# High parts of the self-attention's weights cast on ScalarE in place of GpSimd, with the block sums and the late rows' second round moved

## The reference

```python
x = _layernorm(x + _L0_attn_ref(...));  x = _layernorm(x + _L0_xattn_ref(...))
x = _layernorm(x + _L0_ffn_ref(...))
x = _layernorm(x + _L1_attn_ref(x, L1_attn_weight_qkv, L1_attn_weight_proj), axis=-1)   # here
x = _layernorm(x + _L1_xattn_ref(...)); x = _layernorm(x + _L1_ffn_ref(...))

def _L1_attn_ref(tokens, weight_qkv, weight_proj):
    SEQ, BATCH, HIDDEN = (512, 1, 1024)
    NUM_HEADS, NUM_KV_HEADS, HEAD_DIM = (32, 8, 128)
    Q_PER_GROUP = NUM_HEADS // NUM_KV_HEADS
    ...
    S, B, H = tokens.shape
    qkv = jnp.einsum('sbh,ph->sbp', tokens, weight_qkv)
    qkv = qkv.reshape(S, B, NUM_KV_HEADS, Q_PER_GROUP + 2, HEAD_DIM)
    ...
    scores = jnp.einsum('bhsd,bhtd->bhst', q, k) * scale
    scores = jnp.where(causal, scores, jnp.finfo(scores.dtype).min)
    attn = jax.nn.softmax(scores, axis=-1)
    out = jnp.einsum('bhst,bhtd->bhsd', attn, v)
    out = out.transpose(2, 0, 1, 3).reshape(S, B, NUM_HEADS * HEAD_DIM)
    return jnp.einsum('sbe,he->sbh', out, weight_proj)
```

## Time and profile before

| | |
|---|---|
| median of 3 runs | 3434.92 us (3430.94 to 3437.0) |
| the profiled execution's own time | 3445.45 us |
| its span, first to last instruction | 3443.7 us |
| self-attention, about | 790 to 2745 us of the span |
| TensorE matmuls busy, whole span | 3101.1 us (90%) |
| VectorE, ScalarE, GpSimd busy | 2116.8, 1378.1, 1436.0 us (61%, 40%, 42%) |
| TensorE's mean granted clock | 0.944 of full |

### The profile page before, as it was taken

How to read it: one execution, slowest core, us unless ns; L and a number is a source line. 1 busy time by engine, 2 the same in 40 slices (tenths; PEclk the granted TensorE clock), 3 DMA queues, 4 the chain that set the end, 5 groups by cost and what they waited for, 6 DMA issues and landing times. The chain is left out here.

```text
span 3443.7 us, 70284 instructions
## 1 busy us (share of the span) xinstructions
PE 3101.1 (90%) x26232; PEld 2571.2 (75%) x26232; DVE 2116.8 (61%) x4937; ACT 1378.1 (40%) x3762; POOL 1436.0 (42%) x1423
## 2 busy tenths in 40 slices
PE   5999999984789889988989899999999789999997
PEld 4888888772677778777867787878777568888886
DVE  6788888865454555555554354434444568888886
ACT  3778887763211111111111011101111177787774
POOL 3222222212664656466556766676676300111010
PEclk9999999985899999999989999999999989999999
DMA  9777777622121221122144212121121476656551
GB/s 284 191 189 189 190 190 188 177 74 74 56 71 44 77 71 62 59 89 77 44 162 181 80 56 68 50 68 65 63 77 37 186 180 158 159 148 156 149 139 44
DMA packets 233107, 397.97 MB, mean 116 GB/s; under 512 B 31185, under 2 KB 160817, under 8 KB 232258
## 3 DMA queue, kind: packets, MB, share of 16 engines
q1 hardware_dynamic: 229312, 391.27, 40.3%
q10 hardware_dynamic: 3458, 2.20, 0.2%
HBM read 296.97 MB, written 96.42 MB: 114 GB/s over the span
## 5 line engine op out<-in xcount | busy, mean ns | idle before, releaser
L879 DVE CUSTOM_DVE_ANT_0 L_masked<-L_scores,L_nmask 112x375 f32<-112x375 f32 x1024 | 552.6, 544 | 176.0 <-PE L_scores L483 138.1
L750 ACT ACTIVATE L_probs<-L_masked,L_least 112x375 f32<-112x375 f32 x1024 | 627.9, 615 | 81.1 <-DVE L_least L879 77.2
L1577 PE MATMUL sa_banks<-both_hi,sa_r_hi 128*128 128x420 f32 (+1 forms) x1344 | 500.2, 372 | 47.1 <-POOL sa_r_lo L1430 34.4
L488 PEld LDWEIGHTS L_turned<-ident_sb,L_probs 112*125 112x125 f32 x3072 | 458.2, 190 | 107.6 <-issue 48.0
L488 PE MATMUL L_turned<-ident_sb,L_probs 112*125 112x112 f32 x3072 | 527.3, 281 | 7.4 <-ACT L_probsT L745 3.3
L1910 DVE TENSOR_TENSOR sa_acc<-sa_acc,sa_banks 128x512 f32<-128x512 f32 x448 | 306.9, 687 | 337.8 <-PE sa_banks L1631 336.6
L1577 PE MATMUL sa_banks<-both_lo,sa_r_hi 128*128 128x420 f32 (+1 forms) x1344 | 490.2, 365 | 0.0
L1577 PE MATMUL sa_banks<-both_hi,sa_r_lo 128*128 128x420 f32 (+1 forms) x1344 | 489.5, 364 | 0.0
L1430 POOL TENSOR_TENSOR sa_r_lo<-sa_raw,sa_r_hi 128x512 fp32r<-128x512 f32 (+1 forms) x304 | 466.8, 1536 | 45.2 <-issue 2.3
L483 PE MATMUL L_scores<-L_krep,L_qrep 128*112 128x376 f32 x1024 | 418.6, 410 | 8.4 <-DMA L_qrep<-query_parts 6.6
L745 ACT COPY L_probsT<-L_turned 125x336 f32<-125x336 f32 x768 | 337.3, 439 | 177.4 <-PE L_turned L488 169.2
(11 more groups left out here) (317 smaller groups left out, 5532.5 us busy)
## 6 DMA issues: line engine op xcount, KB each, us to landing
L_qrep<-query_parts SPq DMA_DIRECT2D x256, 224.0 KB, 6.1
sa_raw<-in_wqkvU_dram SPq DMA_DIRECT2D x192, 256.0 KB, 3.2
L_krep<-ctx_parts SPq DMA_DIRECT2D x256, 188.0 KB, 4.2
sa_raw<-in_wprojU_dram SPq DMA_DIRECT2D x128, 256.0 KB, 3.0
query_parts<-L_qT_hi SPq DMA_DIRECT2D x64, 224.0 KB, 6.4
query_parts<-L_qT_lo SPq DMA_DIRECT2D x64, 224.0 KB, 6.8
L_xcur<-x SPq DMA_DIRECT2D x32, 448.0 KB, 5.0
L_val<-in_ctx_dram SPq DMA_DIRECT2D x64, 187.5 KB
```

The source lines that it names most:

```text
L488: mm = pe.transpose(turned[0:TC, m % 2, S * j:S * j + S], probs[0:S, m % 4, TC * j:TC * j + TC], ident[0:S, 0:S])
L750: nc.scalar.activation(probs[0:S, e % 4, :], masked[0:S, e % 4, :], ACT.Exp, bias=least[0:S, e:e + 1], scale=-1.0, accum_out=rsum[0:S, e:e ...
L879: v.tensor_tensor_reduce(out=masked[0:S, n % 4, :], in0=scores[0:S, (NH * t + n) % 3, 0:T], in1=nmask[0:S, :], scale=1.0, scalar=HUGE, op0 ...
L1577: mm = pe.matmul(out_of[o][:, 0:width], a[:, n % RING, k, :], right, start=(o in opens and i == 0), stop=(i == 3 * HALF_KT - 1), skip_grou ...
```

## The change

Four things change, all within `self_attention`; the arithmetic stays the same.

1. The casts of all weights' high parts (pairs and heads) go from GpSimd to ScalarE: `cast_weight(n)` and `cast_head(G, hp, j)`. GpSimd keeps the subtraction (`low`) and waits for the cast with a new semaphore, `cast_ok`; `cast_at` numbers the casts in ScalarE's order. The casts stand in ScalarE's order by `follow(G, pr, o)`: behind the `keep` of product o comes the cast for product o + 4; where heads follow the pair, the casts of the two heads take the places at `B21` and `T3`, and the first four weights of the *next* pair are cast at `T4` (one) and `B22` (three), ahead of `weighted`.
2. GpSimd's block sums stand earlier: a21 + a22 ahead of the first weight of a pair, and the other three each behind the subtraction that they follow. ScalarE waits for them with `mix_ok`.
3. The late rows' second round goes from the pair Q01 to behind the heads: on ScalarE and VectorE it stands within `project(G, 0)`, at chunks 0 to 3.
4. SyncE stores the second round's parts one group later, just ahead of the raw loads of the next group's Q01, and loads the next late row behind them.

```diff
--- before.py
+++ after.py
...
+        def weight_source(G, pr):
+            first = place[G, units(pr)[0], None, 0]
+            a11, a21, a22, a12 = (raw[:, (first + i) % 6, :] for i in range(4))
+            return [x.rearrange("p (k n) -> p k n", k=HALF_KT) for x in (a11, mid[:], mid[:], a12, a11, a22, a12)]
...
                 if u == Q_UNIT + 2 and r is not None:
-                    for n in range(2):
-                        store_parts(r, n)
-                if (u, j) == (None, 0) and r is not None and r + 1 < NC:
-                    load_late(r + 1)
+                    store_parts(r, 0)
+                if u == (K_UNIT if G == NKV else Q_UNIT) and G and late_row(G - 1) is not None:
+                    store_parts(late_row(G - 1), 1)
+                    if r is not None:
+                        load_late(r)
...
-            def split(hi, lo, src, done):
-                p.tensor_copy(hi, src)
-                pool.drain()
+            def low(hi, lo, src, key, done):
+                pool.wait_ge(cast_ok, cast_at[key])
                 p.tensor_tensor(lo, src, hi.bitcast(F32), ALU.subtract).then_inc(done, 1)
 
             def weights(G, pr, start=0, stop=OPS):
                 hi, lo = ring_of(G)
-                ua, ub = units(pr)
-                first = place[G, ua, None, 0]
+                first = place[G, units(pr)[0], None, 0]
                 a11, a21, a22, a12 = (raw[:, (first + i) % 6, :] for i in range(4))
-                source = (a11, mid[:], mid[:], a12, a11, a22, a12)
+                source = weight_source(G, pr)
                 for o in range(start, stop):
                     n = OPS * (3 * G + pr) + o
-                    if n >= RING:
-                        pool.wait_ge(prod_ok, n - RING + 1)
                     if o == B11:
                         loaded(first)
+                        loaded(first + 2)
+                        p.tensor_tensor(mid[:], a21, a22, ALU.add).then_inc(mix_ok, 1)
+                    low(hi[:, n % RING, :, :], lo[:, n % RING, :, :], source[o], ("w", n), w_ok)
                     if o == T1:
-                        loaded(first + 2)
-                        p.tensor_tensor(mid[:], a21, a22, ALU.add)
-                    if o == T2:
                         pool.drain()
-                        p.tensor_tensor(mid[:], mid[:], a11, ALU.subtract)
-                    if o == T3:
+                        p.tensor_tensor(mid[:], mid[:], a11, ALU.subtract).then_inc(mix_ok, 1)
                         pool.drain()
-                        p.tensor_tensor(a11, a11, a21, ALU.subtract)
-                        p.tensor_tensor(a12, a12, mid[:], ALU.subtract)
-                    pool.drain()
-                    split(hi[:, n % RING, :, :], lo[:, n % RING, :, :],
-                          source[o].rearrange("p (k n) -> p k n", k=HALF_KT), w_ok)
+                        p.tensor_tensor(a11, a11, a21, ALU.subtract).then_inc(mix_ok, 1)
+                    if o == B21:
+                        pool.drain()
+                        p.tensor_tensor(a12, a12, mid[:], ALU.subtract).then_inc(mix_ok, 1)
                     if o in (T3, T4, B22):
                         pool.drain().then_inc(raw_free, 2 if o == T3 else 1)
...
             def heads(G, hp):
...
                 hi, lo = heads_of(G, hp)
                 for j in range(2):
-                    split(hi[:, j, :], lo[:, j, :], raw_of(G, None, 2 * hp + j), p_ok)
+                    low(hi[:, j, :], lo[:, j, :], raw_of(G, None, 2 * hp + j), ("p", G, 2 * hp + j), p_ok)
                     pool.drain().then_inc(raw_free, 2)
...
+            def cast_weight(n):
+                m, o = n // OPS, n % OPS
+                G, pr = m // 3, m % 3
+                first = place[G, units(pr)[0], None, 0]
+                if o == B11:
+                    loaded(first)
+                if o == B21 or o == T1:
+                    loaded(first + 2)
+                if o in (T1, T2):
+                    act.wait_ge(mix_ok, 4 * m + o)
+                if o in (T3, B22):
+                    act.wait_ge(mix_ok, 4 * m + 4)
+                if n >= RING:
+                    act.wait_ge(prod_ok, n - RING + 1)
+                if G == NKV and pr == KV and o < RING:
+                    act.wait_ge(proj_ok, heads_done(G - 1, 0))
+                nc.scalar.copy(ring_of(G)[0][:, n % RING, :, :], weight_source(G, pr)[o]).then_inc(cast_ok, 1)
+
+            def cast_head(G, hp, j):
+                if j == 0 and ends_half(G) and hp:
+                    act.wait_ge(prod_ok, OPS * 3 * (G + 1))
+                elif j == 0 and nth[G, hp]:
+                    G0, hp0 = projects[nth[G, hp] - 1]
+                    act.wait_ge(proj_ok, heads_done(G0, hp0))
+                i = place[G, None, 2 * hp + j, 0]
+                loaded(i)
+                nc.scalar.copy(heads_of(G, hp)[0][:, j, :],
+                               raw[:, i % 6:i % 6 + 2, :].rearrange("p x n -> p (x n)")).then_inc(cast_ok, 1)
+
+            def follow(G, pr, o):
+                n = OPS * (3 * G + pr) + o
+                last = pr == Q23 and ends_half(G)
+                owner = (G - 1, 1) if pr == Q01 and late_project(G) else (G, 0) if pr == Q23 else None
+                if o % 2 == 0 and o < B22:
+                    keep(G, pr, o // 2)
+                if owner is None or o < B21:
+                    cast_weight(n + RING)
+                elif o in (B21, T3):
+                    cast_head(*owner, o - B21)
+                elif not last:
+                    cast_weight(n + 2)
+                if owner and o == B22 and not last:
+                    cast_weight(n + 3)
+                    cast_weight(n + 4)
+
...
+                    if hp == 0 and c == 2 and late_row(G) is not None:
+                        high_parts(1, late_row(G), 1)
+                    if ends_half(G) and hp == 0 and c in (3, 4):
+                        cast_head(G, 1, c - 3)
+                    if last and c == 1 and G + 1 < GROUPS:
+                        for first in range(RING):
+                            cast_weight(OPS * 3 * (G + 1) + first)
...
-                keep(G, KV, 0)
-                if late_project(G):
-                    take_exp(G - 1, 1)
-                keep(G, KV, 1)
-                keep(G, KV, 2)
-                if r is not None:
-                    norm(EARLY1 + r, late[:], norm_ok)
-                keep(G, Q01, 0)
-                if r is not None:
-                    copy_turned(1, r)
-                    high_parts(1, r, 0)
-                keep(G, Q01, 1)
-                keep(G, Q01, 2)
-                if r is not None:
-                    high_parts(1, r, 1)
+                for o in range(OPS):
+                    follow(G, KV, o)
+                    if o == T1 and late_project(G):
+                        take_exp(G - 1, 1)
+                    if o == T4 and r is not None:
+                        norm(EARLY1 + r, late[:], norm_ok)
+                for o in range(OPS):
+                    follow(G, Q01, o)
+                    if o == B11 and r is not None:
+                        copy_turned(1, r)
+                        high_parts(1, r, 0)
                 if late_project(G):
                     weighted(G - 1, 1)
-                keep(G, Q23, 0)
-                values(G)
-                take_exp(G, 0)
-                keep(G, Q23, 1)
-                keep(G, Q23, 2)
+                for o in range(OPS):
+                    follow(G, Q23, o)
+                    if o == B11:
+                        values(G)
+                    if o == T1:
+                        take_exp(G, 0)
                 weighted(G, 0)
...
+                    if hp == 0 and c == 0 and late_row(G) is not None:
+                        differences(1, late_row(G), 1)
+                    if hp == 0 and c == 3 and late_row(G) is not None:
+                        low_parts(1, late_row(G), 1)
...
-                combine(G, Q01, 0)
-                if r is not None:
-                    differences(1, r, 1)
-                combine(G, Q01, 1)
-                if r is not None:
-                    low_parts(1, r, 1)
-                combine(G, Q01, 2)
-                combine(G, Q01, 3)
+                for n in range(4):
+                    combine(G, Q01, n)
```

21 lines of the change are left out of this document (13 added, 8 removed).

## The result

The changed kernel takes 3570.6 us (median of 4 runs, 3566.0 to 3574.3) against 3436.0 (4 runs, 3430.9 to 3437.6): 3.9% slower, ratio 1.039 (95% interval 1.038 to 1.041).

A forecast was written before the change was run, and what follows sets the result against it. TensorE was taken as the bound, so only its waits count. Terms 31 + 55 + 7 + 9 - 3 + 1 + 1.5 + 26 = 128 us gave 3573 on the profiled 3445.5, or 3563 on the median 3434.9; range 3510 to 3625.

The forecast's parts named there:

- What goes: Ahead of products at T3: TensorE's 34.4 us of waits for GpSimd's low parts should be gone without GpSimd's casts.
- The new wait: Projections after Q23: `weigh` held by ScalarE's queued casts, +5.2 us each in groups 1 to 6, +9.1 in 9 to 14.
- K + 11.7: Start of the second `weigh` after the change, 11.7 us behind K, the start of ScalarE's third `kept` copy.
- Late row: Projection after Q01, groups 1 to 7: `weigh` +1.3 us later each (-0.8 to +2.6), 9 us in all.
- The second round in `project(G, 0)`: ... 0: Late row's three casts and three subtractions moved into that projection: no cost, at most 1 us for seven groups uncovered.
- +1, with ScalarE held once in `project(7, 1)`: Group 8: the expert block's delay less three T3 waits, +1 us in all, ScalarE held once in that projection.
- Clock: The 12 projections after Q23: mostly at full clock before, not after the longer waits, 2.2 us each, 26 us.
- The start: Start of the stage: GpSimd's first block waits for ScalarE, which delays the first roots, +1.5 us.
- ScalarE is not held, faster: Rival: casts ahead of the projection find `mid` ready, so existing waits and low clock shrink, 3296 us; 5%.
- The second rival: Raw loads in late groups and expert blocks hide: late groups take 15 us less, second half 35 less, 3513 us; 12%.
- the third: Rival: low clock lasts longer, or ScalarE is late for `kept` in late groups, 3616 us; 23%.
- The fourth: Rival: gains at T3 and in the late groups equal the added wait, so time stays at 3435 us; 3%.

The follow-up runs named there:

- e1: The changed kernel with the casts of T2 and B21 moved behind the casts into `o_hi` of chunk 3: 3437.2 us, 0.999 of the kernel before.
- e2: The changed kernel with T1's cast behind `o_hi` of chunk 2, T2's and B21's behind that of chunk 3: 3342.5 us, 0.972 of the kernel before.
- e4: The kernel before with only the late rows' second round and its stores moved behind the heads, casts left on GpSimd: 3417.1 us, ratio 0.993.
- e8: The changed kernel with SyncE issuing group 8's four raw weight loads ahead of the reload of the tokens: 3549.2 us, 1.032 of the kernel before.
- e7: The changed kernel with the late row's second round back in Q01, leaving the casts and GpSimd's order: 3594.1 us, 1.046 of the kernel before.
- e6: e2 with group 8's casts at chunks 5 and 6, normalizations after the loop, late rows' first-round stores behind Q23's raw loads: 3296.6 us, 0.959 of the kernel before.
- e9: e2 with the late rows' first-round stores behind Q23's raw loads, and e8's move: 3292.4 us, 0.957 of the kernel before.

## Why the prediction was right

The stage went from 1,860.2 to 1,986.7 us, +126.4; the start gave -5.1 and the stage behind -0.8. I split each stage, from the starts and durations of TensorE's matmuls, into gaps between its pieces (163.2 before, 287.9 after) and the time that pieces took beyond the same piece at full clock (78.2 and 86.8). The two give +133; the other -7 is mostly the overlap of neighbouring matmuls, which a gap that goes gives back.

| term | forecast | measured |
|---|---|---|
| gaps, groups 1 to 6: the new wait after Q23 and the late row | 6 x (5.2 + 1.3) = 39 | 37.5 |
| gaps, groups 9 to 14: expert block, and after Q01 | 6 x (9.1 + 1.0) = 61 | 59.1 |
| group 0, whole length | -3 | -3.9 |
| gaps, group 7 | 1 | about +21 |
| group 8, whole length | +1 | +6.1 |
| group 15, whole length | +1 | +0.7 |
| low clock, groups 1 to 7 and 9 to 14 | 26 | +9 |
| start | +1.5 | -5.1 |

The measured column adds up to 124; the other 4 us down to 120.5 are overlap in groups 1 to 7 and 9 to 14 (3) and the stage behind (0.8).

*What goes.* Right: no wait for GpSimd at T3 is left, and a weight costs ScalarE 0.62 us and a head 1.05, against 0.60 and 1.10 taken.

*The new wait.* Right to 0.1 us where it could be read (K + 11.74 in group 4 after Q23 and K + 11.70 in group 13 after Q01, against K + 11.7), 6.3 to 6.8 us against 6.5 after Q23 in the first half, 10.0 to 10.2 against 10.4 in the second. e1 and e2 show that its cause is the one named, queue order: with the casts of T2 and B21 elsewhere 133 us are back.

*Late row.* +1.3 each was forecast, from group 4's rows. There the gaps ahead of and in that projection are 10.9 us (0.7 + 10.2) where they were 9.2 (2.05 + 5.8 + 1.3), +1.7. Over the seven places it is +0.8 on average, from -0.3 in group 3 to +2.6 in group 2: in groups 1, 3, 5 and 7 the wait for `qT` before was 7.3 us and not group 4's 5.8, which the working left out. VectorE's low parts ran at 0.59 to 0.62 us with GpSimd idle and 1.58 to 1.60 with GpSimd at work; in six of the seven groups one of the first round's four was slow, so most of that part of the bound was used.

*Step that failed: "The second round in `project(G, 0)`: ... 0" and group 8's "+1, with ScalarE held once in `project(7, 1)`".* I asked only what VectorE and ScalarE do there. Six of seven times that is right, but the last late row's stores end the chain that lets the tokens be reloaded, 12.5 MB at 420 GB/s and 30 us long, and in front of group 8's weights. e4 shows the wait without the casts, e8 takes it away by one order on SyncE.

*Also missed: group 8, +1 forecast, +6.1 measured.* In its Q01 ScalarE stands 7.90 us for raw weights, and the copy of `kept` stands behind that cast:

```profile
1928.89 0.62 ACT L1731 CAST sa_r_hi<-sa_raw 128x512 fp32r<-128x512 f32 x1 [7.90 <-DMA sa_raw<-in_wqkvU_dram]
```

VectorE's sum into `qT` waits for the copy, and TensorE 4.2 us for the sum (the wait for `sa_qT` in the result's rows). Before, no cast stood ahead of `kept`. It is the same kind of loss as in the projections; no run was made on it alone, and e7 and e8 have it too (4.2 us each).

*Step mis-sized: "Clock. The 12 projections after Q23 mostly started at full clock and will not ...: 2.2 each, 26 us".* By their first chunks only 7 of the 12 were at full clock before (3.04 to 3.06 us; the other five took 4.5 to 4.6). After, all twelve take 4.8 to 5.5, 19 us more than before in sum, and other places got some of that back, where T3 and `qT` no longer wait: +9 net in these groups. This miss and that of group 7 (20 us the other way) nearly cancel, so the sum of 128 against the measured 120.5 looks better than its terms; that part is luck. Nor is 120.5 exact: by the medians the difference is 134.7, since the profiled execution before lies 9.5 us above its median of 4 runs and the one after 4.7 below.

*The start.* It went the other way than forecast: the self-attention's first product comes at 874.1 and not 879.2, 5.1 us earlier and not 1.5 later, perhaps since ScalarE's casts there took more off GpSimd than they delayed its roots. No run was made on it.

*The rivals.* "ScalarE is not held, faster", 3296 us at 5%, is not what the change did, but e2, e6 and e9 reach 3342, 3297 and 3292 by bringing about its condition: the casts that wait for `mid` no longer stand ahead of `o_hi`. Its price was worked out rightly: in e6's profile the gaps are 87 us less than before and the low clock 50 (91 and 48 in the rival), though e6 and e9 changed the stores and the half's end as well, and e2 without that stays at 3342. The second rival (loads and expert block hidden) is shown false by group 12's rows. Of the third, TensorE's waits for `kept` come to 3.0 us in all, the longest 0.9, and the low clock to +9, so neither half came. The fourth is shown false by the gaps.

## What to carry to other kernels

When work is moved to an idle engine, its busy share says nothing; list what is queued behind each new wait, and who waits for that. A cast that waits for another engine's result belongs behind the short one that TensorE is about to ask for: here the place of three casts per projection was worth 228 us of 3,571. And follow a moved store to the last of its kind: what is reloaded once all are stored starts when the last one lands, and everything behind it in the DMA queue is late by as much.

## What the runs showed of the hardware

Behind one and the same gap of 1.3 us, TensorE runs the next chunk at full clock (3.05 us, granted 1.00) in one execution and mostly at 1.2 GHz (4.6 us, granted 0.61) in another of the same program; in the changed kernel, behind gaps of 6 to 11 us, that chunk always took 4.2 to 5.5 us. Two profiles of one program gave clock losses of 28.0 and 33.3 us, of another 36.8 and 34.5, so one profile gives them to within 5 us or so, not better.

VectorE's low part with two inputs in SBUF (128x256) took 0.62 us while GpSimd stood and 1.60 beside its work, in one and the same late row of the changed kernel. By the Trainium skill, page SBUF — State Buffer, section Who interferes with whom, a VectorE instruction with two SBUF inputs contends with a GpSimd instruction that reads SBUF; the rows agree.

```profile
1372.11 0.62 DVE L1905 TENSOR_TENSOR both_lo<-sa_late,both_hi 128x256 fp32r<-128x256 f32 x1
...
1373.65 1.60 DVE L1905 TENSOR_TENSOR both_lo<-sa_probsT,both_hi 128x256 fp32r<-128x256 f32 x1
```
